# Score matmuls of the first attention in row tiles of 32 rows, one run per pass, the second pass's run directly behind the attends

## The reference

```python
q = (x @ Wq + bq).reshape(B, S, NH, HD)     # 16 heads of 8
k = (x @ Wk + bk).reshape(B, S, NH, HD)
v = (x @ Wv + bv).reshape(B, S, NH, HD)
q = _l2norm(q)
k = _l2norm(k)
state = q
for _ in range(2):
    sim = jnp.einsum('bqhd,bkhd->bqhk', state, k)
    att = jax.nn.softmax(sim, axis=-1)
    state = jnp.einsum('bqhk,bkhd->bqhd', att, v)
o = state.reshape(B, S, H) @ Wo + bo
return residual + o
```

## Time and profile before

| | us |
|---|---|
| median of 3 runs | 1747.61 (1747.36 to 1748.15) |
| profiled execution, its own time | 1759.47 |
| its span (first to last instruction of the program) | 1757.7 |
| PE busy / weight loads busy | 1489.7 (85%) / 1147.2 (65%) |
| DVE busy | 1189.0 (68%) |
| ACT busy | 1000.8 (57%) |
| POOL busy | 785.2 (45%) |
| first attention: copies of `ot` (L558), first and last start | 64.7 and 585.8, one in each step |
| score matmuls L395, first pass | 512, mean 298 ns, 59.2 to 559.8 of the span |
| score matmuls L395, second pass | 512, mean 286 ns, 85.6 to 582.7 of the span |

### The profile page before, as it was taken

The page is one execution under the profiler, slowest core; times in us unless marked ns, Lnnn a source line. Parts: engine busy times, 40 slices in busy tenths (PEclk is TensorE's granted clock), DMA queues, the critical chain, the costliest instruction groups (busy, mean ns, idle before and its releaser), DMA issues. The chain is left out here.

```text
span 1757.7 us, 37146 instructions
## 1 busy us (share of the span) xinstructions
PE 1489.7 (85%) x12057; PEld 1147.2 (65%) x12057; DVE 1189.0 (68%) x3253; ACT 1000.8 (57%) x1682; POOL 785.2 (45%) x1008
## 2 busy tenths in 40 slices
PE   2599999999999587999169998999899999689997
PEld 1467767767766466899046666666666666478886
DVE  2367777767766555999556777777777766556676
ACT  1377777777776254777126565665656666333332
POOL 8765464685662343998562334343333220100111
PEclk9899999999999788999569999999999999789999
DMA  5000000010010110222211111111111111000000
GB/s 192 21 20 19 16 19 17 25 32 19 25 35 19 33 58 12 73 68 64 77 42 35 35 35 40 31 35 33 33 33 33 31 30 30 1 1 7 12 12 18
DMA packets 75074, 60.29 MB, mean 34 GB/s; under 512 B 17088, under 2 KB 71104, under 8 KB 74560
## 3 DMA queue, kind: packets, MB, share of 16 engines
q1 hardware_dynamic: 70848, 50.21, 10.0%
q0 software_dynamic: 4096, 8.40, 1.7%
HBM read 20.01 MB, written 13.37 MB: 19 GB/s over the span
## 5 line engine op out<-in xcount | busy, mean ns | idle before, releaser
L1274 DVE TENSOR_REDUCE a_qt<-a_ps_d 128x2 fp32r<-128x512 f32 (+1 forms) x384 | 263.6, 689 | 140.8 <-PE a_ps_d L1059 96.3
L537 ACT ACTIVATE a_p<-a_ps_s 128x1024 f32<-128x1024 f32 x256 | 263.1, 1029 | 63.8 <-PE a_ps_s L395 59.4
L638 DVE TENSOR_REDUCE a_qt<-a_ps_d 128x2 fp32r<-128x512 f32 x256 | 171.6, 685 | 105.8 <-PE a_ps_d L406 105.5
L799 POOL TENSOR_TENSOR a_rn<-a_ss,a_half 128x16 f32<-128x16 f32 x64 | 185.9, 2913 | 1.4
L1186 ACT ACTIVATE a_pg<-a_ps_s 128x1024 f32<-128x1024 f32 x128 | 131.8, 1031 | 12.5 <-PE a_ps_s L1033 7.4
L1059 PE MATMUL a_ps_d<-a_kpad,a_qs 128*128 128x512 f32 x256 | 126.2, 493 | 13.6 <-DVE a_qt L1274 12.5
L406 PE MATMUL a_ps_d<-a_kpad,a_qs 128*128 128x512 f32 x256 | 119.7, 471 | 15.5 <-DVE a_qt L638 13.9
L413 PE MATMUL a_ps_o<-a_p,a_v 128*32 128x256 f32 x2048 | 125.3, 384 | 1.0 <-ACT a_p L537 1.0
L1024 PE MATMUL a_ps_a<-ident,a_qt 128*128 128x128 f32 x512 | 107.1, 291 | 10.8 <-ACT a_qsm L1180 8.0
L1505 POOL COPY a_v<-a_vt 128x64 f32<-128x64 f32 x64 | 15.4, 240 | 212.8 <-PE a_ps_o L1136 212.8
L1180 ACT CAST a_ks<-a_ps_a 128x256 fp32r<-128x256 f32 x128 | 47.6, 372 | 110.0 <-PE a_ps_a L1024 101.7
(11 more groups left out here) (359 smaller groups left out, 4280.1 us busy)
## 6 DMA issues: line engine op xcount, KB each, us to landing
a_kpad<-a_ks SPq DMA_DIRECT2D x512, 32.0 KB, 1.8
a_kpad<-a_kq SPq DMA_DIRECT2D x256, 32.0 KB, 1.9
f_xin<-xs SPq DMA_DIRECT2D x39, 128.0 KB, 2.1
ys<-f_yout SPq DMA_DIRECT2D x39, 128.0 KB, 2.1
w<-in_w SPq DMA_DIRECT2D x2, 2304.0 KB, 11.3
out_x<-X SPq DMA_DIRECT2D x8, 256.0 KB, 2.3
xs<-f_zero SPq DMA_DIRECT2D x15, 128.0 KB
wgu<-in_wgu SPq DMA_DIRECT2D x1, 1152.0 KB
```

Of the source, the lines that this page charges most:

```text
L537: nc.scalar.activation(probs[:, u % 2, 2 * c:2 * c + 2, :, :].rearrange("p a b c -> p (a b c)"), ps_s[:, n % 2, :], ACT.Exp).then_inc(exp_ ...
L638: nc.vector.tensor_reduce(qt2[:, k % 2, 2 * part:2 * part + 2, SHIFT], bank(k, f"m{part}")[:, :].rearrange("p (a b) -> p a b", b=S), AX.X, ...
L799: nc.gpsimd.tensor_tensor(rn[:, part * c:(part + 1) * c], ss[:, part * c:(part + 1) * c], half[:, 0:c], ALU.pow).then_inc(rn_ready, 1)
L1274: nc.vector.tensor_reduce(dst, src, AX.X, ALU.max, negate=True).then_inc(d_done, 1)
```

## The change

`ps_s` becomes four banks, one per head. The eight score matmuls of a pass are written as one run, in which each reads the 32 rows of its head only, from `kpad` and from the query (row tiles); four that follow each other use four different row tiles and four different banks. The first pass's run stands where chunk 0 stood. The second pass's run moves to directly behind the attends, ahead of m0. Since one run fills all four banks, each run waits for both exponentials of the run before it. On ACT exponential 3 now stands ahead of the KQ copy, and exponentials 0 and 1 wait for the same run, 2 and 3 too.

```diff
-        ps_s = pb("ps_s", [P, 2, 1024])
+        ps_s = pb("ps_s", [P, G, TPB * S])
...
-            def score_chunk(st, which, q):
-                u = st.k if which < 2 else st.k - 3
-
-                wait(pe, exp_done, st.at(lambda k: chunks(k, which) - 2))
-                n = chunks(st.k, which) - 1
-                for jj in range(2):
-                    j = 2 * (which % 2) + jj
-                    for t in range(TPB):
-                        last = nc.tensor.matmul(ps_s[:, n % 2, jj * 512 + t * S:jj * 512 + (t + 1) * S],
-                                                kpad[:, u % RING, j, t * P:(t + 1) * P], q, start=True, stop=True)
+            def scores(u, q):
+
+                for t in range(TPB):
+                    for j in range(G):
+                        rows = slice(SLOT * j, SLOT * (j + 1))
+                        last = nc.tensor.matmul(ps_s[:, j, t * S:(t + 1) * S],
+                                                kpad[rows, u % RING, j, t * P:(t + 1) * P], q[rows, :],
+                                                start=True, stop=True)
                 last.then_inc(scores_full, 1)
...
                     pe.wait_ge(a_done, a_count(k - NG, "KQ"))
-                    score_chunk(st, 0, kq[:, k % KQ_RING, 1, :])
+                    wait(pe, exp_done, exps_of(k - 1, 3))
+                    scores(k, kq[:, k % KQ_RING, 1, :])
                 if projects:
                     pe.wait_ge(a_done, a_count(k - 1, "xT"))
                     project(st, 0, "qp")
-                if unit(k):
-                    score_chunk(st, 1, kq[:, k % KQ_RING, 1, :])
...
                 if a_live(k, "T"):
                     pe.wait_ge(a_done, a_count(k, "T"))
+                if unit(k - 3):
+                    pe.wait_ge(exp_done, exps_of(k, 1))
+                    scores(k - 3, qs2[:, S:2 * S])
                 maxima(st, 0)
...
-                if unit(k - 3):
-                    score_chunk(st, 2, qs2[:, S:2 * S])
                 maxima(st, 1)
...
                 maxima(st, 2)
-                if unit(k - 3):
-                    score_chunk(st, 3, qs2[:, S:2 * S])
                 maxima(st, 3)
...
             def exps(st, which, u, probs):
-                act.wait_ge(scores_full, chunks(st.k, which))
+                act.wait_ge(scores_full, scored(st.k, which // 2))
...
                 if unit(k - 3):
                     exps(st, 2, k - 3, p2)
+                if unit(k - 3):
+                    exps(st, 3, k - 3, p2)
                 if unit(k + NG):
                     copy_a(st, "KQ", kq[:, (k + NG) % KQ_RING, :, :].rearrange("p a s -> p (a s)"), slice(0, 2 * S))
-                if unit(k - 3):
-                    exps(st, 3, k - 3, p2)
```

More of the change, by code:

```diff
@@ L339, in halves, with exps_of @@
             return slice(0 if first else S, 2 * S if second else S)
-        def chunks(k, which):
+        def exps_of(k, which):
             n = 2 * clip(k, UNITS) + 2 * clip(k - 3, UNITS)
@@ L345, in chunks, with scored @@
             return n + sum(order[:which + 1])
+        def scored(k, half):
+            return clip(k, UNITS) + clip(k - 3, UNITS) + unit(k) + half * unit(k - 3)
         def bn_count(k, which):
@@ L366, in _ @@
                 if k - NG >= 0:
-                    hold(sp, scores_full, st.at(lambda k: chunks(k - 1, 3)), passed)
+                    hold(sp, scores_full, st.at(lambda k: scored(k - 1, 1)), passed)
                 u = k + NG
@@ L460, in _ @@
                     if unit(k - 4):
-                        pe.wait_ge(exp_done, chunks(k - 1, 3))
+                        pe.wait_ge(exp_done, exps_of(k - 1, 3))
                         last = attend(k - 4, p2, 1)
                     if unit(k - 1):
-                        pe.wait_ge(exp_done, chunks(k - 1, 1))
+                        pe.wait_ge(exp_done, exps_of(k - 1, 1))
                         pe.wait_ge(v_ready, k)
@@ L531, in exps @@
             def exps(st, which, u, probs):
-                act.wait_ge(scores_full, chunks(st.k, which))
+                act.wait_ge(scores_full, scored(st.k, which // 2))
                 if which % 2 == 0:
                     wait(act, o_full, attends(st.k - 1))
-                n = chunks(st.k, which) - 1
                 c = which % 2
                 nc.scalar.activation(probs[:, u % 2, 2 * c:2 * c + 2, :, :].rearrange("p a b c -> p (a b c)"),
-                                     ps_s[:, n % 2, :], ACT.Exp).then_inc(exp_done, 1)
+                                     ps_s[:, 2 * c:2 * c + 2, :].rearrange("p a b -> p (a b)"),
+                                     ACT.Exp).then_inc(exp_done, 1)
             def copy_a(st, task, dst, live=slice(0, S)):
```

## The result

The changed kernel takes 1791.67 us (1790.41 to 1793.16, four runs) beside 1747.86 for the kernel before on the same chip: ratio 1.0251, 95% interval 1.0234 to 1.0269. It is slower by 43.8 us where 21.2 were forecast; the time lies inside the range, the size of the loss is twice the forecast's.

What follows compares the result with a forecast made beforehand. The prediction took a ring of waits between PE and DVE in the first attention as the bound. Terms of 20.7 and 3.5, less 2.6 and 0.4, gave +21.2 us on 1747.6: 1768.8 us, range 1756 to 1796.

Steps and rivals of the forecast that it cites:

- The ring: First attention: T (transposes), attends, m0 (first maxima matmul), DVE's maxima and division set each step; PE matters only T to m0.
- Row tiles side by side: Second-pass run between attends and m0: open load 0.10, two groups 0.24, border 0.10, together 0.44 us a step.
- B: Rival, score runs: row tiles don't overlap, each run takes 1.06; +68 us, 1816 us, chance 0.07.
- two at a time: Rival, score runs: only two row tiles overlap, 0.68 a step; +35 us, 1783 us, chance 0.08.
- r = 3: Steps where PE is late for T: T about 0.5 sooner, but the moved run waits for exponential 1, m0 0.25 later.
- What POOL takes back: At r = 2, DVE's wait for POOL's powers absorbs 0.88 of the delay in three steps: 2.6 us back.
- the last step: Last step of the first attention: the old run of eight stood open ahead of two exponentials, so -0.4 us.
- the Sum: Whole kernel: 20.7 plus 3.5, less 2.6 and 0.4, gives +21.2 us; later stages start behind and don't change.
- outside r = 3 this earns nothing: First pass's run, 0.34 in place of 0.96: PE only reaches T's wait earlier, so no gain except where r = 3.
- C: Rival, first attention: exponential 1 ends too late everywhere, 0.2 more in each of 62 steps; +12 us, 1781 us, chance 0.08.
- A: Rival, first attention: PE is the bound after all, so less PE work makes it faster; -58 us, 1689 us, chance 0.09.
- D: Rival, first attention: the shift is absorbed by unseen slack, within 0.2%; 1748 us, chance 0.04.

Runs made afterwards that it cites:

- e4: Changed kernel with the second pass's row-tiled run moved back behind m0: 1767.04 us beside 1748.18, ratio 1.0102.
- e10a: Kernel before with the second of each head's two first-pass score matmuls left out, from step 8, except where r = 3: ratio 1.0000.
- e10b: Kernel before with the second of each head's two score matmuls left out in both passes, from step 8, except where r = 3: ratio 0.9997.
- e2: Changed kernel with both passes' score runs over all 128 rows, at the changed places: 1814.02 us, ratio 1.0375.
- e1: Changed kernel with only the first pass's run back over all 128 rows: 1781.85 us beside 1748.18, ratio 1.0196.
- f4: The changed kernel itself run again, unaltered, on another chip: 1788.25 us, ratio 1.0227.
- f3: Changed kernel with throwaway matmuls added as row-tiled ones, ahead of the first pass's run (not where r = 3) and ahead of O: 1782.07 us, ratio 1.0185.
- e5: Changed kernel with the second pass's row-tiled run behind m0 and the first pass's run over all 128 rows: 1761.49 us, ratio 1.0073.
- f runs: Changed kernel repeated, with row-tiled filler, or with full-row scores half left out, second run ahead of or behind m0: ratios 1.0227, 1.0185, 1.0189, 1.0016.

## Why the prediction was half right

- **The ring, and PE off it but from T to m0.** Held, in its length; that PE's work off the ring costs nothing did not (below). m0 stands 2.87 behind T (305.07 to 307.94), forecast 2.85; T still follows L759 by 0.15; e4, with the run off the ring, restores 2.42. e10a and e10b show that full-row scores elsewhere can be halved for no gain.
- **Row tiles side by side, 0.44 a step.** Held. The moved run takes 0.44 to m0's start. Its two groups of four are further apart than the 0.12 I took: the first four start together, the last four within 0.3. The source view of L396, for 325.1 to 325.2 and for 325.2 to 325.6 us:

```profile
L396 PE MATMUL a_ps_s<-a_qs,a_kpad x4: 351/382/384, 325.1 to 325.1; 32*128 32x256 f32 x4
...
L396 PE MATMUL a_ps_s<-a_qs,a_kpad x8: 273/312/384, 325.1 to 325.4; 32*128 32x256 f32 x8
```

  The sum was right, the split within it not, so that the exact 0.44 is in part luck. Rivals B and "two at a time" are out. By the Trainium skill's 3.07 times (TensorE: Matmul & The Clock Gate, Part 3) a run of 0.96 would take an estimated 0.31. Here e2's open run took 1.03 and the row-tiled one 0.44, each up to the next matmul's start: 2.3 times, and that is what counts for this kernel.
- **r = 3, 0.25.** The moved run does start right behind ACT's exponential 1. Timeline of ACT, then of PE, one such step:

```profile
323.95 1.04 ACT L536 ACTIVATE a_p<-a_ps_s 128x1024 f32<-128x1024 f32 x1
```

```profile
325.14 0.51 PE L396 MATMUL a_ps_s<-a_qs,a_kpad 32*128 32x256 f32 x8
325.57 0.50 PE L408 MATMUL a_ps_d<-a_kpad,a_qs 128*128 128x512 f32 x1
```

  323.95 + 1.04 = 324.99, and 0.15 later the run, where I had 0.06; m0 came 0.32 later for the forecast 0.25. T came 0.33 sooner (0.57 behind L759 in place of 0.90), not 0.5, which changed nothing, as the run waits for ACT. A whole undisturbed batch came to +1.59 for the forecast 1.57.
- **What POOL takes back, the last step.** Small: DVE's `scaled` waits 13.3 us for POOL in place of 17.0, 3.7 less, for 2.6 expected.
- **The step that failed is the Sum**: it ends in +21.2 and "later stages start behind this one and don't change", and it prices every matmul at the full clock that rows 1 show. The later stages indeed did not change. But the trace before proves a clock of 1.00 only for the PE stream before. The change takes PE's stream from 463 to 413 busy us of 495, puts the scores in row tiles, and takes T's wait from 8.4 to 28.9. The term that is missing is 14 stretches at 1.2 GHz, about 22 us, measured above. The sentence "outside r = 3 this earns nothing" about the first pass's run failed with it: e1 shows that run's shortness to cost 5 to 10 us. The range holds the time by luck: its upper part was there for C and "two at a time" and a margin, not for the clock.
- **Rivals.** A is out by e10b, C by T to m0 (nothing holds the run where r is not 3), D by the result. None of them named the clock. The two with a time near the result, "two at a time" at 1783 and C at 1781, are the wrong mechanisms.

## What to carry to other kernels

First find the ring of instructions that wait for each other, and price a move by what it puts on that ring; a faster instruction off it earns nothing, and a shared wait ("one run per pass") may put all of it on. Then ask what the saved PE work does to the granted clock: with the scores in row tiles, the half-clock stretches cost as much here as the move itself, while the same saving in full rows at the old places cost nothing. If a change makes PE's work lighter, look at the clock column of its windows before explaining anything else, and test with filler.

## What the runs showed of the hardware that I had not expected

- The half clock comes in separate stretches inside a loop in which PE is busy 84% by the records (413.46 of 495.00), 14 and 10 in two executions of one kernel, mostly in other steps each time.
- Eight row-tiled matmuls of 32 rows by 256 columns, four at a time, take 0.44 us from their start to the next matmul's; eight full-row ones 1.03.
- Throwaway matmuls made a kernel faster: 1.0227 in the same job without, 1.0185 with (f4 and f3, 1788.25 and 1782.07 us).
- One kernel differs by 10 us between chips: the kernel before took 1748 to 1749 us in the jobs of the result, of e1 to e5 and of the f runs, and 1757.57 and 1758.78 on the chip of the others. The difference lay behind the first attention: from the last `ot` copy to the end all profiles of the first kind take 1158 to 1160 us, all of the second 1165 to 1174 (the profile of the kernel before 1172). Only ratios on one chip are compared here.

## What stays open

Whether the row-tiled form itself brings the half clock, or the shorter time that PE really works in it, was not separated; that form and amount of work both bear on it is argued from counts and mean clocks, not shown by one run. Why a stretch falls into one step and not into its twin isn't known either. Whether the 48 us at 1.2 GHz at the end of e4 have the same cause was not tried.
